# A perceiver block on one core: a second loop in a new order, with the attention scores computed after the first feed-forward's first layer

## What is computed

```python
x = x + xattn0(ctx, layernorm(x))          # softmax cross-attention
x = x + mamba(layernorm(x))                # gated selective scan
x = x + ffn0(layernorm(x))                 # "c": 256 -> 1024, gelu, layernorm, 1024 -> 256, ternary weights
x = x + xattn1(layernorm(x), ctx)          # "d": focused linear attention, 16 heads
x = x + attn1(layernorm(x))                # "e": latent attention with decay, 16 heads, 32 keys
x = x + ffn1(x)                            # "f"/"h": two bitlinear layers, rmsnorm, int8 activations
# the query of "d":  q = relu(h @ Wq + bq) + 1e-6;  q = q / softplus(scale)
#   q = q**3 / |q**3| * |q|;  out = (q . kv) / (q . ksum + 1e-6)
```

## Time and profile before

| | |
|---|---|
| median of 3 runs (lowest, highest) | 2238.33 us (2237.59, 2258.23) |
| profiled execution, its span | 2234.23 us, 2232.4 us |
| busy PE, DVE, ACT, POOL | 83%, 71%, 66%, 54% |
| mean granted TensorE clock | 0.928 |
| second loop's prologue | about 1403 to 1430 us |
| second loop, first statistics to the end | 1430 to 2232 us |

### The profile page before, as it was taken

The page is one execution under the profiler, slowest core; times in us unless marked ns, Lnnn a source line. Parts: engine busy times, 40 slices in busy tenths (PEclk is TensorE's granted clock), DMA queues, the critical chain, the costliest instruction groups (busy, mean ns, idle before and its releaser), DMA issues. The chain is left out here.

```text
span 2232.4 us, 41590 instructions
## 1 busy us (share of the span) xinstructions
PE 1853.6 (83%) x14324; PEld 1242.3 (56%) x14355; DVE 1592.1 (71%) x2945; ACT 1477.1 (66%) x3431; POOL 1209.7 (54%) x1300
## 2 busy tenths in 40 slices
PE   4899889989989899899899865368888888988874
PEld 2665555555555555565565422256666666666752
DVE  3348777767867867868678686457888878788763
ACT  2558877878868868878778766124656666666654
POOL 1435655545546555545545533156777777677751
PEclk9999999999999999999999986679989999899875
DMA  7322122212221111212121110100000000000000
GB/s 179 121 74 76 44 69 70 62 55 67 68 71 59 63 62 60 64 57 79 43 69 41 38 47 5 54 7 9 13 12 12 12 12 12 12 12 12 10 9 10
DMA packets 48370, 103.20 MB, mean 46 GB/s; under 512 B 6384, under 2 KB 25072, under 8 KB 43376
## 3 DMA queue, kind: packets, MB, share of 16 engines
q1 hardware_dynamic: 48240, 101.57, 14.4%
HBM read 93.03 MB, written 8.52 MB: 45 GB/s over the span
## 5 line engine op out<-in xcount | busy, mean ns | idle before, releaser
L861 POOL TENSOR_TENSOR kcube<-kcube,ksq 128x512 f32<-128x512 f32 x128 | 178.3, 1393 | 474.2 <-ACT ksq L718 474.2
L696 ACT ACTIVATE abuf<-delta,cols 128x496 f32<-128x496 f32 x512 | 338.5, 699 | 30.5 <-DVE gP L943 14.5
L871 POOL TENSOR_TENSOR yac<-yac,gP 128x1024 f32<-128x1024 f32 x128 | 302.3, 2362 | 11.2 <-ACT gP L705 10.1
L943 DVE TENSOR_TENSOR_SCAN gP<-abuf,ps_s 128x512 f32<-128x512 f32 x256 | 293.3, 1196 | 0.6 <-POOL yac L871 0.6
L524 PE MATMUL ps_kv<-kcube,cx 128*128 128x256 f32 x1024 | 249.3, 387 | 40.3 <-ACT kcube L736 39.4
L943 DVE TENSOR_TENSOR_SCAN gL<-abuf,ps_s 128x512 f32<-128x512 f32 x192 | 223.3, 1207 | 57.3 <-ACT abuf L696 57.1
L512 PE MATMUL ps_kv<-w_k,cT 128*128 128x256 f32 x1024 | 255.6, 392 | 0.0
L524 PEld LDWEIGHTS ps_kv<-kcube,cx 128*128 128x128 f32 x1024 | 191.8, 192 | 100.7 <-ACT kcube L736 63.0
L570 PE MATMUL ps_t<-gL,diag 128*128 128x512 f32 x384 | 192.1, 624 | 54.3 <-DVE gL L943 49.0
L512 PEld LDWEIGHTS ps_kv<-w_k,cT 128*128 128x128 f32 x1024 | 184.4, 190 | 49.3 <-issue 29.4
L583 PE MATMUL ps_kv<-hT,w_pT 128*128 128x512 f32 x384 | 186.9, 610 | 18.8 <-ACT delta L769 14.5
(11 more groups left out here) (312 smaller groups left out, 4253.0 us busy)
## 6 DMA issues: line engine op xcount, KB each, us to landing
cT<-in_h_ctxT SPq DMA_DIRECT2D x32, 1028.0 KB, 4.9
cx<-in_ctx SPq DMA_DIRECT2D x32, 1024.0 KB, 5.5
xT<-in_h_xT SPq DMA_DIRECT2D x8, 512.0 KB, 3.7
xcur<-in_x SPq DMA_DIRECT2D x32, 128.0 KB, 2.0
x_mid<-xb SPq DMA_DIRECT2D x16, 256.0 KB, 2.2
x_c<-x_mid SPq DMA_DIRECT2D x32, 128.0 KB, 2.0
out<-y SPq DMA_DIRECT2D x32, 128.0 KB, 1.7
kv_all<-vleft SPq DMA_DIRECT2D x8, 256.0 KB, 10.5
```

What stands on the lines that cost most here:

```text
L696: act.activation(abuf[q % 2][:, i, :].rearrange("p (b t) -> p b t", t=T)[:, :, 1:T], delta[J % 2][:, :].rearrange("p (b t) -> p b t", t=T) ...
L861: pool.tensor_tensor(t[:, :, :], t[:, :, :], ksq[:, :, :], ALU.mult).then_inc(S["k3_ready"], 1)
L871: pool.tensor_tensor(yac[:, :, :], yac[:, :, :], pool_home(q)[:, :, :], ALU.add).then_inc(S["pacc_done"], 1)
L943: dve.tensor_tensor_scan(dst[:, i, :], abuf[q % 2][:, i, :], ps_u[:, :], 0.0, ALU.mult, ALU.add).then_inc(S["scan_done"], 1)
```

## The change

All of it is in the second loop and its prologue. The same values are computed, but for one detail: softplus and bias are folded into the query's weights and a bias matmul, so that one DVE operation (`max`) is left of two. Its core, cut. In the prologue, on DVE (behind these lines the bias is split into three bfloat16 pieces, as lines L342 to L350 of the first loop's prologue do it for the key):

```diff
-            dve.tensor_scalar(W["bq"], W["bq"], K_EPS, None, ALU.add)
+            dve.tensor_tensor(W["wq"][:, :, :], W["wq"][:, :, :], isp[:, :].unsqueeze(1).broadcast_to([P, DC, D]), ALU.mult)
+            dve.tensor_scalar(W["epi"][:, :], isp[:, :], K_EPS, None, ALU.mult)
+            link(dve.scalar_tensor_tensor(out=W["bq"], in0=W["bq"], scalar=K_EPS, in1=isp[:, :], op0=ALU.add, op1=ALU.mult))
```

In `pe_body`. The order at the start of a step is now: turn qcube, turn he, turn gn, the numerators of d, p times v. The scores `e_sc` come behind `c_fc`:

```diff
+        if e1 is not None:
+            pe.wait_ge(S["e_h"], e1 + 1)
+            turn(ps_e1, he[:, :], DC, ident[:, :]).then_inc(S["e_turn"], 1)
...
             pe.wait_ge(S["d_hT"], d1 + 1)
+            pe.matmul(ps_d[:, 0:D], W["ones_b"][0:3, :], W["qbias"][0:3, :], start=True, stop=False)
...
-        if e1 is not None:
-            pe.wait_ge(S["e_km"], e1 + 1)
...
-            last.then_inc(S["e_sc"], 1)
         if c1 is not None:
             pe.wait_ge(S["c_hT"], c1 + 1)
...
             last.then_inc(S["c_fc"], 1)
+        if e1 is not None:
+            pe.wait_ge(S["e_km"], e1 + 1)
...
+            last.then_inc(S["e_sc"], 1)
         if c2 is not None:
             pe.wait_ge(S["c_gT"], 2 * (c2 + 1))
```

In `act_body` the second square of d (`d_s6`) goes ahead of the two gelu operations of c. In `pool_body`:

```diff
-        if e1 is not None:
-            root("e", sm["e_mv"][:, 1:2], ln_eps, "e_var", e1 + 1, "e_rstd")
...
+        if c1 is not None:
+            root("c", sm["c_mv"][:, 1:2], ln_eps, "c_var", c1 + 1, "c_rstd")
         if d1 is not None:
...
-        if c1 is not None:
-            root("c", sm["c_mv"][:, 1:2], ln_eps, "c_var", c1 + 1, "c_rstd")
...
+        if d2 is not None:
+            root("e", sm["e_mv"][:, 1:2], ln_eps, "e_var", d2 + 1, "e_rstd")
         if c1 is not None:
+            root("g", sm["g_mv"][:, 1:2], ln_eps, "c_bn", c1 + 1, "c_gr")
...
             pool.tensor_tensor(x_p[:, :], x_c[:, :], W["crow"][:, :], ALU.add).then_inc(S["c_xpc"], 1)
-            root("g", sm["g_mv"][:, 1:2], ln_eps, "c_bn", c1 + 1, "c_gr")
```

In `dve_body` the norm gn now opens the step, the reciprocals and o_e of e come behind hq, hc_lo ahead of x5, and:

```diff
-            dve.tensor_tensor(kq[:, :], ps_d[:, 0:D], W["bq"], ALU.add).then_inc(S["d_kb"], 1)
+            dve.tensor_tensor(kq[:, :], ps_d[:, 0:D], W["epi"][:, :], ALU.max).then_inc(S["d_kf"], 1)
...
-        if d1 is not None:
-            dve.wait_ge(S["d_kb"], d1 + 1)
-            dve.scalar_tensor_tensor(out=kq[:, :], in0=kq[:, :], scalar=K_EPS, in1=isp[:, :], op0=ALU.max, op1=ALU.mult).then_inc(S["d_kf"], 1)
+        if d2 is not None:
+            dve.wait_ge(S["d_t"], d2 + 1)
...
+            dve.tensor_tensor(x4[:, :], t_d2[:, :], t_d[:, :], ALU.add).then_inc(S["x4"], 1)
+            dve.wait_ge(S["x4"], d2 + 1)
+            dve.bn_stats(sm["e_bn"][:, :], x4[:, :]).then_inc(S["e_bs"], 1)
+            dve.wait_ge(S["e_bs"], d2 + 1)
+            apart(dve)
+            dve.bn_aggr(sm["e_mv"][:, :], sm["e_bn"][:, :]).then_inc(S["e_var"], 1)
...
+        if d1 is not None:
+            dve.wait_ge(S["d_r"], d1 + 1)
+            dve.tensor_scalar(qcube[:, :], qcube[:, :], sm["rr"][:, 0:1], sm["rr"][:, 1:2], ALU.mult, ALU.mult).then_inc(S["d_qf"], 1)
         if d2 is not None:
...
+            dve.wait_ge(S["e_turn"], d2)
+            norm("e", x4[:, :], he[:, :], "e_rstd", d2 + 1, "e_h")
```

More of the change, by code:

```diff
@@ L1352, in pe_body @@
             turn(ps_d, qcube[:, :], DC, ident[:, :]).then_inc(S["d_qturn"], 1)
+        if e1 is not None:
+            pe.wait_ge(S["e_h"], e1 + 1)
+            turn(ps_e1, he[:, :], DC, ident[:, :]).then_inc(S["e_turn"], 1)
+        if c2 is not None:
+            pe.wait_ge(S["c_gn"], c2 + 1)
+            for hh in range(2):
+                last = turn(ps_cf[:, hh, :], gn[:, hh * 512:(hh + 1) * 512], 4, ident[:, :])
+            last.then_inc(S["c_gturn"], 1)
+        if d2 is not None:
+            pe.wait_ge(S["d_qfT"], d2 + 1)
+            pe.wait_ge(S["d_blk"], 2 * (d2 + 1))
+            for c in range(DC):
+                for b in range(GB):
+                    last = pe.matmul(ps_d[b * T:(b + 1) * T, c * (P + HH):(c + 1) * (P + HH)], qfT[:, c, b * T:(b + 1) * T],
+                                     blk[:, b, c, :], start=True, stop=True)
+            last.then_inc(S["d_num"], 1)
         if e2 is not None:
@@ L1406, in pe_body @@
             pe.wait_ge(S["d_hT"], d1 + 1)
+            pe.matmul(ps_d[:, 0:D], W["ones_b"][0:3, :], W["qbias"][0:3, :], start=True, stop=False)
             for dc in range(DC):
-                last = pe.matmul(ps_d[:, 0:D], hdT[:, dc, :], W["wq"][:, dc, :], start=(dc == 0), stop=(dc == 1))
+                last = pe.matmul(ps_d[:, 0:D], hdT[:, dc, :], W["wq"][:, dc, :], start=False, stop=(dc == 1))
             last.then_inc(S["d_q"], 1)
@@ L1457, in pe_body @@
             last.then_inc(S["c_fc"], 1)
+        if e1 is not None:
+            pe.wait_ge(S["e_km"], e1 + 1)
+            pe.wait_ge(S["e_kmd"], e1 + 1)
+            pe.wait_ge(S["e_v"], e1 + 1)
+            for c in range(DC):
+                for b in range(GB):
+                    last = pe.matmul(ps_e1[b * T:(b + 1) * T, c * D:(c + 1) * D], qTe[:, c, b * T:(b + 1) * T],
+                                     kTm[:, c, b, :, :].rearrange("p h k -> p (h k)"), start=True, stop=True)
+            last.then_inc(S["e_sc"], 1)
         if c2 is not None:
@@ L1532, in act_body @@
             act.activation(hf[:, :], hp[:, :], ACT.Gelu).then_inc(S["f_h"], 1)
+        if d1 is not None:
+            act.wait_ge(S["d_k3"], d1 + 1)
+            act.activation(ksq[:, :], qcube[:, :], ACT.Square, accum_out=sm["s26"][:, 1:2]).then_inc(S["d_s6"], 1)
         if c1 is not None:
@@ L1640, in norm @@
             dve.tensor_scalar(h, x, sm[k + "_mv"][:, 0:1], sm[k + "_r"][:, 0:1], ALU.subtract, ALU.mult).then_inc(S[done], 1)
-        if d2 is not None:
-            dve.wait_ge(S["d_r"], d2 + 1)
-            dve.tensor_scalar(qcube[:, :], qcube[:, :], sm["rr"][:, 0:1], sm["rr"][:, 1:2], ALU.mult, ALU.mult).then_inc(S["d_qf"], 1)
+        if c2 is not None:
+            norm("g", ga[:, :], gn[:, :], "c_gr", c2 + 1, "c_gn")
         if e2 is not None:
@@ L1660, in dve_body @@
             dve.tensor_scalar(sm["h_m"][:, :], sm["h_mx"][:, :], sm["h_r"][:, 0:1], 1e-5, ALU.mult, ALU.max).then_inc(S["h_m"], 1)
[L1661 to L1674, removed]
+        if f1 is not None:
+            dve.wait_ge(S["x5"], f1 + 1)
+            dve.tensor_reduce(sm["f_mx"][:, :], x5[:, :], AX_X, ALU.max, apply_absolute_value=True).then_inc(S["f_max"], 1)
         if f2 is not None:
@@ L1702, in dve_body @@
             dve.tensor_scalar(hq[:, :], hf[:, :], sm["h_qs"][:, 0:1], MAGIC, ALU.mult, ALU.add).then_inc(S["f_hqd"], 1)
+        if e2 is not None:
+            dve.wait_ge(S["e_av"], e2 + 1)
+            dve.reciprocal(sinv[:, :].unsqueeze(2), heads(ps_e2[:, 0:H * (HD + 1)])[:, :, HD:HD + 1]).then_inc(S["e_rs"], 1)
+            dve.wait_ge(S["e_rs"], e2 + 1)
+            dve.tensor_tensor(heads(o_e[:, :]), heads(ps_e2[:, 0:H * (HD + 1)])[:, :, 0:HD],
+                              sinv[:, :].unsqueeze(2).broadcast_to([P, H, HD]), ALU.mult).then_inc(S["e_o"], 1)
+        if c1 is not None:
+            dve.wait_ge(S["c_in"], 16 * (c1 + 1))
+            dve.bn_stats(sm["c_bn"][:, :], x_c[:, :]).then_inc(S["c_bs"], 1)
         if f1 is not None:
@@ L1745, in dve_body @@
                                      op1=ALU.add).then_inc(S["f_y"], 1)
-        if d1 is not None:
-            dve.wait_ge(S["d_kb"], d1 + 1)
-            dve.scalar_tensor_tensor(out=kq[:, :], in0=kq[:, :], scalar=K_EPS, in1=isp[:, :], op0=ALU.max, op1=ALU.mult).then_inc(S["d_kf"], 1)
+        if c1 is not None:
+            dve.wait_ge(S["c_hi"], c1 + 1)
+            dve.tensor_tensor(hc_lo[:, :, :], halves(ps_c1[:, 0:D]), hc_hi[:, :, :].bitcast(F32), ALU.subtract).then_inc(S["c_hT"], 1)
         if e2 is not None:
```

58 lines of the change are left out of this document (26 added, 32 removed).

## The result

The changed kernel takes 2260.68 us (median of 20 runs) against 2239.98: ratio 1.0083, interval [1.0064, 1.0102]. The forecast was 2232, with 2256 as its upper end.

The account below looks back on a forecast made before the run. DVE's tail behind x5 and PE's matmuls behind hc_lo were taken to bound the step together. Hardware loop 0, prologue +4.1, fill -4.4, drain -5.8 gave -6.1 us on 2234.23, so 2228.1; median 2232, range 2203 to 2256.

Parts of the forecast that it names:

- PE is outside of the loop: Hardware loop: c_fc no longer waits for scores or x5, so PE's projection ends before DVE's tail; PE idle 3.86 us.
- the clock term: Hardware loop: slow clock adds at most 1.33 us a step through gn's transposes and d's numerators; 0.45 taken, giving 22.19.
- x3 to c's statistics: Hardware-loop step, on DVE: from x3 to the end of c's statistics 6.50 us, between 6.1 and 6.9; 8.11 before.
- Statistics to kTm: Hardware-loop step, on POOL: new wait for the root of c, then root, blk, t_d; 3.94 us, between 3.7 and 4.5.
- kTm to x5: Hardware-loop step: from POOL's kTm to DVE's x5, claimed unchanged at 3.88 us.
- x5 to x3: Hardware-loop step, DVE's tail: hc_lo goes out, statistics of e, qcube and he come in; 7.42 us, between 7.1 and 7.8.
- Prologue: Before the hardware loop: nine added DVE instructions and a 128x512 product, one dropped; +4.1 us, covered by nothing.
- Fill: Filling steps: scores behind c_fc cover their 2.22 us wait for POOL's kTm; two steps, -4.4 us (0 to -10).
- Drain: Draining steps: hq now ahead of p times v, 1.94 us on the chain; three steps, -5.8 us (0 to -10).
- The slower rival: Hardware loop: slow clock reaches the latent projections, kTe late, kTm to tail shift; 22.94 a step, +18 us, 2250; chance 0.17.
- The bound is PE: Hardware loop: PE stays the bound, waits of 0.89 and 1.01 us go; 20.29 a step, -45.6 us, 2187; chance 0.08.
- the "right" list: Hardware-loop signs of a right forecast: POOL waits about 2 us, DVE unwaited x5 to x3, PE idle gathered, 22 us step.

## Why the prediction was wrong, step by step

**The step that failed: "PE is outside of the loop", and with it the clock term.** The sum at full clock, 21.74, was measured as 21.82. On it I put 0.45 us for the clock; 1.47 was measured. The 1.02 between them, times 24, is 24.5 of the 35.3 us by which the profiled execution missed its 2228.1; the fill, below, is most of the rest. I priced the slow clock only where DVE waits for gn's turn and the numerators, since the scores seemed to come long before DVE needs them. They don't. By moving e_sc behind c_fc the change put all of PE's matmuls but the projection and two turns into one run without a pause, between x3 and sc_s. The rows had it: PE busy 17.88 at full clock and 20.58 at 0.85, less the projection 3.62 and the turns 0.88, is 13.4 and 16.1 us. With the 1.9 us ahead of gn's turn and the 5.7 from sc_s to x3, both read only afterwards, this is 21.0 and 23.7: short of 21.74 at full clock, 2 us over it at 0.85. I had ruled out a PE bound by its total, at full clock alone.

Shown, not argued: the changed order takes 23.29 us a step; with the clock held it takes 21.83, with the scores first 22.28, with both 21.62. So the scores' place costs 0.21 us a step at full clock and 1.01 with the falls.

**The other terms.**

- *x3 to c's statistics*: 6.90 (forecast 6.50). gn beside x_p took 1.33, not 0.78 and 0.29.
- *Statistics to kTm*: 4.61 (3.94). The wait was as forecast, 2.23 us against "about 2", but t_d took 1.60, not 0.62, beside DVE's half of kTm.
- *kTm to x5*: 2.73 (3.88). POOL's kTm took 1.91 instead of 2.87, since DVE's half no longer ran beside it.
- *x5 to x3*: 7.58 (7.42), with 0.12 between hp and sc_s, which starts 0.07 after the scores' end. The four deviations (+0.40, +0.67, -1.15, +0.16) cancel to 0.08 by luck.
- *Prologue*: +4.1 forecast. The first statistics of c start 4.2 us later (1433.73, 1429.54). DVE's operations ahead of them take 23.73 us (from 1405.69) against 19.86 (from 1405.60), 3.87 more; then both wait for the DMA of x_c, 4.31 and 4.08 us. So the term is right to 0.2 us. From trace to trace the start itself moves more, with the end of the first loop: 1431.77 to 1445.65 in those with the new prologue.
- *Fill*: -4.4 forecast, +3.2 measured (150.1 against 146.9 us). The wait of PE for kTm is gone, but DVE gets one for the scores: 4.67 us in the fifth step, the first that has scores, and 3.26 in the sixth. Timeline of DVE there:

```profile
1533.83 0.69 DVE L1768 TENSOR_TENSOR sc_s<-ps_m,decay 128x512 f32<-128x512 f32 x1 [3.26 <-PE ps_m L1472]
```

- *Drain*: -5.8 forecast, -4.6 measured (118.8 against 123.5 us).

**The rivals.** The slower rival was the right one in what happens: the clock falls through the latent projections, and kTe comes at 11.53 us after x3 in the step at 0.86 (9.04 at 1.00), so that kTm waits 1.00 us for it. It gave 22.94 a step and 2250; 23.29 and 2261 were measured. But by its own path (kTe, kTm, x5) DVE reaches hp's end 1.17 us before the scores, so its price was taken on the wrong wait. The decisive one was PE's queue. "The bound is PE" had a rival of its own at 0.08, only as a gain. Of the signs named, POOL's wait ahead of the root of c (2.23 us) and kTm waiting for kTe both came, one for "right" and one for "slower"; the "right" list also had DVE without a wait from x5 to x3, and its wait of 1.17 us for the scores there is the mark of the step that failed.

**The rule on the clock.** PE idles 1.96 and 1.33 us in each step of after, where it idled 0.89 and 1.01 before, and the mean clock was 0.91 in both loops. In all, a full-clock step leaves PE idle 3.50 us (21.82 - 18.32), less than the 3.86 forecast and the 3.72 of before. The Trainium skill (TensorE: Matmul & The Clock Gate, "HAM oscillation") says that idle time between groups of matmuls sends the clock to half rate anew each time. In that page's case the waits are longer than the matmuls between them; here they are a small part of the step, and that the clock falls even so is shown by this case's traces. By that rule the two kernels alike have falls, and the unread matmuls remove them; the traces agree with both. It says nothing of where they are waited for, and that was the loss here.

**The rule on the port.** gn started at 1866.90 and x_p at 1866.96; x_p took 0.72, as it did with x_p moved, and gn 1.33, 0.52 longer than there. The Trainium skill (SBUF — State Buffer, "SBUF: two separate sides") has the later instruction blocked. By it x_p would have begun when gn ended; the trace differs here, the one that is shown as earlier lost. The starts lie 0.06 us apart and POOL's spans are rough, so which of the two had the port first is not shown. With hc behind blk (2.01 us, done 0.16 after blk) it is the later one that waits, as the page says.

**Open.** Why the clock falls in every step with x_p moved and the scores last, in every third with the scores first, and in every second with the scores first and x_p unmoved, the runs don't tell; PE's idle time ahead of qcube's turn differs (1.96 and 1.37 us), but no run varied it alone.

## What to carry to other kernels

Before a piece of an engine's queue is moved, add up that engine's whole run between the event that starts it and the result that another engine waits for, at each clock that the trace shows, and not only its share of the step. Independent work put ahead of a result that others wait for joins their critical path, even if it seems to fit into their slack at full clock (0.21 us a step here at full clock, 1.01 with the falls); and slack is also what absorbs the falls of the clock. An edit that gains nothing in one order (x_p moved, 1.0109 with the scores last) can gain 0.9% in another (0.9984 to 0.9898): it is worth a second try once the bound has moved.

## What the runs showed of the hardware

- 26 matmuls of 256 columns that nobody reads, in PE's idle time, hold the granted clock at 1.00 over 24 steps and gain 35 us there, though PE is busy 36 us more (511.92 against 475.92).
- Work on POOL lengthens work on DVE and the other way round by up to 1.66 us, most of the partner's duration: hq 0.75 alone, 2.41 beside blk (2.06); hc 2.01 beside blk (1.92), 0.70 where blk is done before; t_d 0.61 alone, 1.60 beside DVE's kTm; POOL's kTm 1.91 alone, 2.87 beside it.
- A pattern of falls can lock in: 21 steps at 23.89 us within 0.01, the clock 0.86.
- The same time lost to the clock on PE reaches the step in different parts, by where PE's work is waited for: 0.40 of it before, 0.97 after.
